# Rounding constant of a weight quantizer from a two-byte ScalarE magnitude, and nearly every second unit's second-half product in three passes

## Time and profile before

| | |
|---|---|
| time before, median of 3 runs | 833.17 us (832.89 to 833.23) |
| the profiled execution's own time | 833.1 us |
| its span, first to last instruction | 831.3 us |
| stage 1, up to the last hidden and project products | about 381 us |
| stage 2 | the rest |
| granted TensorE clock | 1.00 throughout |
| busy: PE, DVE, ACT, POOL | 825.8, 479.5, 345.9, 511.8 us |

### The profile page before, as it was taken

The page is one execution under the profiler, slowest core; times in us unless marked ns, Lnnn a source line. Parts: engine busy times, 40 slices in busy tenths (PEclk is TensorE's granted clock), DMA queues, the critical chain, the costliest instruction groups (busy, mean ns, idle before and its releaser), DMA issues.

```text
span 831.3 us, 10181 instructions
## 1 busy us (share of the span) xinstructions
PE 825.8 (99%) x3568; PEld 479.9 (58%) x3568; DVE 479.5 (58%) x499; ACT 345.9 (42%) x372; POOL 511.8 (62%) x238
## 2 busy tenths in 40 slices
PE   9999999999999999999999999999999999999998
PEld 5777777776767676765444444444444444444444
DVE  6989889788888888888553232323232323232322
ACT  7999999988888888973100000000000000000000
POOL 2899999899999999995983242424242423232322
PEclk9999999999999999999999999999999999999999
DMA  7988999877777877657974868686868686868682
GB/s 258 322 321 321 367 339 353 301 285 296 284 289 303 305 267 301 253 187 246 298 295 119 282 214 282 210 285 212 280 213 280 214 283 214 279 213 282 215 248 107
DMA packets 75008, 220.77 MB, mean 266 GB/s; under 512 B 37594, under 2 KB 40930, under 8 KB 55778
## 3 DMA queue, kind: packets, MB, share of 16 engines
q1 hardware_dynamic: 74080, 219.30, 74.5%
q10 hardware_dynamic: 898, 1.09, 0.4%
HBM read 143.04 MB, written 69.21 MB: 255 GB/s over the span
## 4 chain that ended last, share of the span: by engine, by line
PE 99%; issue 0%; POOL 0%; DVE 0%; ACT 0%; POOLq 0%
PE ps_h L1071 53%; PE ps_h L980 22%; PE ps_o L995 11%; PE ps_o L1011 8%; PE ps_o L1007 4%; PE ps_o L934 1%; PE ps_h L1047 0%; PE ps_o L1071 0%; PE ps_o L980 0%; PE ps_o L1065 0%; POOL time L518 0%; PE ps_o L940 0%; PE ps_h L1052 0%; DVE o_and_max L881 0%; ACT x_sb L702 0%
## 5 line engine op out<-in xcount | busy, mean ns | idle before, releaser
L1071 PE MATMUL ps_h<-wqT,x_sb 128*128 128x512 bf16 x1920 | 413.7, 378 | 0.2 <-ACT x_sb L702 0.2
L1071 PEld LDWEIGHTS ps_h<-wqT,x_sb 128*128 128x128 fp8e5 x1920 | 187.7, 98 | 224.4 <-ACT x_sb L702 0.3
L528 POOL TENSOR_TENSOR xl<-x_sb,xh 128x1024 fp32r<-128x1024 f32 x62 | 149.5, 2411 | 16.3 <-ACT xh L607 16.3
L980 PE MATMUL ps_h<-xh,whl 128*128 128x512 f32 x508 | 150.3, 417 | 0.4
L569 POOL TENSOR_TENSOR x_sb<-x_sb,bias_sb 128x2048 f32<-128x2048 f32 (+1 forms) x15 | 66.7, 4447 | 131.7 <-DMA x_sb<-in_x 131.7
L569 POOL TENSOR_TENSOR h<-h,bias_sb 128x2048 f32<-128x2048 f32 (+1 forms) x15 | 66.7, 4443 | 122.7 <-DMA h<-in_x 122.7
L881 DVE SCALAR_TENSOR_TENSOR o_and_max<-ps_h,scales,h 128x512 f32<-128x512 f32 (+1 forms) x59 | 44.0, 746 | 136.2 <-PE ps_h L1071 136.2
L881 DVE SCALAR_TENSOR_TENSOR o_and_max<-ps_h,scales,x_sb 128x512 f32<-128x512 f32 x59 | 44.2, 750 | 133.4 <-PE ps_h L1071 133.4
L980 PEld LDWEIGHTS ps_h<-xh,whl 128*128 128x128 f32 x508 | 94.2, 188 | 42.0 <-issue 21.7
L765 DVE SCALAR_TENSOR_TENSOR o_and_max<-ps_o,b_sb,steps 128x1024 f32<-128x1024 f32 (+1 forms) x65 | 82.2, 1264 | 29.0 <-PE ps_o L1011 27.1
L755 DVE TENSOR_TENSOR hl<-ps_h,hh 128x1024 fp32r<-128x1024 f32 x63 | 76.8, 1219 | 13.4 <-ACT ps_h L614 13.3
(11 more groups left out here) (101 smaller groups left out, 657.2 us busy)
## 6 DMA issues: line engine op xcount, KB each, us to landing
x_sb<-in_x SPq DMA_DIRECT2D x44, 1024.0 KB, 5.7
masked_out<-o_and_max SPq DMA_DIRECT2D x32, 1024.0 KB, 6.8
o_in<-masked_out SPq DMA_DIRECT2D x32, 1024.0 KB, 8.9
out<-o_and_max SPq DMA_DIRECT2D x27, 1024.0 KB, 5.1
wqT<-in_L_ffn_weight SPq DMA_DIRECT2D x23, 684.0 KB, 8.3
wt<-in_L_ffn_weight SPq DMA_DIRECT2D x40, 384.0 KB, 5.5
h<-in_x SPq DMA_DIRECT2D x14, 1024.0 KB, 7.2
whl<-split_w SPq DMA_DIRECT2D x18, 256.0 KB, 6.0
```

The source lines that it names most:

```text
L528: pool.tensor_tensor(xl[:, u % 2, :], x_cols(u), xh[:, u % 2, :].bitcast(fp32), ALU.subtract)\
L980: mm = nc.tensor.matmul(to[:, cols], whl[:, b % SLOTS_W, rows], xs[:, u % 2, cols], start=(k == 0), stop=(k == 2))
L1071: mm = nc.tensor.matmul(bank, q[:, k // 2, :, k % 2], wq[:, n, k, cols], start=(k == 0), stop=(k == KT - 1))
```

## The change

- The rounding constant comes another way. ACT's `scale_chunk` writes `wc = |wt * w_up|` in bf16, with `w_up` = `w_scale` * 2^20 (one small DVE operation more). DVE's `add_round_at` floors `wc` in place, as one contiguous run of 768 bf16 elements, and then makes `ws = wt * w_scale + wc` with one `scalar_tensor_tensor`, which reads `wt` and `wc` in SBUF. `exponents`, `round_at`, `wE` and POOL's addition (L535) go; POOL keeps the subtraction.
- `SPLIT_H1` has one unit more (27), and `QUANT` is one larger (27), so 34 chunks are early and nine late.
- `SPLIT_BEHIND`: the odd units from 29 to 61, 17 of them, run project1 in three passes too. ACT runs two Gelus for them (one to `hh1_behind`, one in place in PSUM); DVE, not POOL, makes the low half `hl1_behind` from PSUM right behind the mask, and scans `o` at the end of its iteration instead of ahead of the chunk. hidden(u+1, 1) waits for the low half.
- SP loads a chunk's buffer again after the DVE addition (`w_added`) instead of after ACT's scaling. ACT scales chunk 36 ahead of its copies at the beginning of stage 2. The late chunks are spread anew on DVE and POOL.

```diff
-    ROUND_AT = 1.5 * 2.0 ** 20
+    ROUND_AT = 2.0 ** 20
-    SPLIT_H1 = [u for u in range(2, 27)]
+    SPLIT_H1 = [u for u in range(2, 28)]
+    SPLIT_BEHIND = [u for u in range(29, UNITS - 2, 2)]
-    QUANT = SCANS + 2
+    QUANT = SCANS + 3
-    CHUNK_BEHIND = range(4, 12)
+    CHUNK_BEHIND = (2, 4, 5, 6, 7)
+        hh1_behind = sb_at("hh1_behind", [P, 2, UNIT], fp32r, h1_at)
+        hl1_behind = sb_at("hl1_behind", [P, UNIT], fp32r, raw_at)
...
@@ SyncE
                     if i >= 3:
-                        sp.wait_ge(w_scaled, i - 2)
+                        sp.wait_ge(w_added, i - 2)
                     load_chunk(i)
@@ GpSimd
             def round_chunk(i):
                 v, c = ws[:, i % 2, 0:chunk_cols(i)], wc[:, i % 2, 0:chunk_cols(i)]
-                pool.wait_ge(w_round_ready, i + 1)
-                pool.tensor_tensor(v, v, c, ALU.add).then_inc(w_added, 1)
                 pool.wait_ge(w_added, i + 1)
                 pool.tensor_tensor(wqT[:, CHUNK_AT[i]], v, c, ALU.subtract).then_inc(w_rounded, 1)
...
@@ ScalarE
                 act.wait_ge(h1_psum, u + k + 1)
+                if u in SPLIT_BEHIND:
+                    act.activation(hh1_behind[:, u % 2, :], ps_h[:, 1, :], ACT.Gelu, bias=hbias[:, 1, b:b + 1])
+                    act.activation(ps_h[:, 1, :], ps_h[:, 1, :], ACT.Gelu, bias=hbias[:, 1, b:b + 1])\
+                       .then_inc(h1_gelu, 1)
+                    return
...
-                act.activation(ws[:, i % 2, 0:chunk_cols(i)], wt[:, at:at + chunk_cols(i)], ACT.Copy, scale=w_scale)\
-                   .then_inc(w_scaled, 1)
+                act.activation(wc[:, i % 2, 0:chunk_cols(i)], wt[:, at:at + chunk_cols(i)], ACT.Abs, scale=w_up)\
+                   .then_inc(w_raised, 1)
...
+            scale_chunk(EARLY_CHUNKS + 2)
@@ VectorE
+            def split_h1_behind(u):
+                dve.wait_ge(h1_gelu, u + 1)
+                if u == SPLIT_BEHIND[0]:
+                    dve.wait_ge(wl_later, DIRECT - UPB)
+                dve.tensor_tensor(hl1_behind[:, :], ps_h[:, 1, :], hh1_behind[:, u % 2, :].bitcast(fp32), ALU.subtract)\
+                   .then_inc(hl1_behind_ready, 1)
...
+            def add_round_at(i):
+                c, at = wc[:, i % 2, 0:chunk_cols(i)], i % 3 * CHUNK
+                dve.wait_ge(w_raised, i + 1)
+                dve.tensor_scalar(c, c, 1.5 * E4M3_MIN_NORMAL * ROUND_AT, None, ALU.max).then_inc(w_floored, 1)
+                dve.wait_ge(w_floored, i + 1)
+                dve.scalar_tensor_tensor(ws[:, i % 2, 0:chunk_cols(i)], wt[:, at:at + chunk_cols(i)], w_scale, c,
+                                         ALU.mult, ALU.add).then_inc(w_added, 1)
...
                     mask_o(u - 1, start, 0, slice(0, UNIT))
+                    if u in SPLIT_BEHIND:
+                        split_h1_behind(u)
...
-                    scan_o(u - 1, 0, slice(0, UNIT))
+                    if u not in SPLIT_BEHIND:
+                        scan_o(u - 1, 0, slice(0, UNIT))
                 if 0 <= u - QUANT - 1 < EARLY_CHUNKS + 1:
-                    exponents(u - QUANT - 1)
-                if 0 <= u - QUANT - 1 < EARLY_CHUNKS:
-                    round_at(u - QUANT - 1)
+                    add_round_at(u - QUANT - 1)
                 if u + 1 < UNITS:
                     split_h_rest(u + 1)
+                if u in SPLIT_BEHIND:
+                    scan_o(u - 1, 0, slice(0, UNIT))
@@ TensorE
                     pe.wait_ge(h1_gelu, u)
+                    if u - 1 in SPLIT_BEHIND:
+                        pe.wait_ge(hl1_behind_ready, SPLIT_BEHIND.index(u - 1) + 1)
...
+                elif u in SPLIT_BEHIND:
+                    for j, (w, hs) in enumerate(((w2l1, hh1_behind[:, u % 2, :]), (w2h1, hh1_behind[:, u % 2, :]),
+                                                 (w2h1, hl1_behind))):
+                        for cols in halves:
+                            mm = nc.tensor.matmul(ps_o[:, u % 2, cols], w[:, :], hs[:, cols],
+                                                  start=False, stop=(j == 2))
```

More of the change, by code:

```diff
@@ L11, in adaln_ffn @@
     fp32r = mybir.dt.float32r
-    u16 = mybir.dt.uint16
     ALU, ACT, AX = mybir.AluOpType, mybir.ActivationFunctionType, mybir.AxisListType
@@ L30, in adaln_ffn @@
     E4M3_MAX, E5M2_MAX, EPS = 448.0, 57344.0, 1e-12
-    EXPONENT = 0x7F80
     E4M3_MIN_NORMAL = 2.0 ** -6
-    ROUND_AT = 1.5 * 2.0 ** 20
+    ROUND_AT = 2.0 ** 20
     assert C == P and UPB == 2 and HT == 2 and weight.shape == (P, WCOLS)
@@ L47, in adaln_ffn @@
     SLOTS = 5
-    CHUNK, CROWS = 768, 3
+    CHUNK = 768
     CHUNKS = -(-WCOLS // CHUNK)
-    QUANT = SCANS + 2
+    QUANT = SCANS + 3
     EARLY_CHUNKS = UNITS - 3 - QUANT
@@ L120, in adaln_ffn @@
         o_max = sb("o_max", [P, UNITS + 1], fp32)
-        scales = sb("scales", [P, 10], fp32)
+        scales = sb("scales", [P, 11], fp32)
         w_pmax, w_rec, w_scale, w_inv = (scales[:, k:k + 1] for k in range(4))
-        o_pmax, o_amax, o_rec, o_scale, o_inv, y_scale = (scales[:, k:k + 1] for k in range(4, 10))
+        o_pmax, o_amax, o_rec, o_scale, o_inv, y_scale, w_up = (scales[:, k:k + 1] for k in range(4, 11))
         wqT = sb("wqT", [P, WCOLS], bf16)
         x_sb = sb("x_sb", [P, 2, T], fp32)
+        raw_at = -(-nc.sbuf_base // 32) * 32
         raw = sb("raw", [P, SLOTS_W, HID], fp32)
+        assert SLOTS_W * HID == UNIT
         whl = sb("whl", [P, SLOTS_W, 2 * HID], fp32r)
@@ L137, in adaln_ffn @@
         hl = sb("hl", [P, 2, UNIT], fp32r)
+        h1_at = -(-nc.sbuf_base // 32) * 32
         h1 = sb("h1", [P, 2, UNIT], fp32)
@@ L146, in adaln_ffn @@
         ws = sb("ws", [P, 2, CHUNK], fp32)
-        wE = sb("wE", [P, CROWS * (CHUNK // CROWS + 2)], u16)
         wc = sb("wc", [P, 2, CHUNK], bf16)
@@ L236, in adaln_ffn @@
         hl1_ready = sem("hl1_ready")
+        hl1_behind_ready = sem("hl1_behind_ready")
         hl_ready = sem("hl_ready")
@@ L250, in adaln_ffn @@
         wt_loaded = [sem(f"wt_loaded{r}") for r in range(3)]
-        w_scaled = sem("w_scaled")
-        w_exponent = sem("w_exponent")
-        w_round_ready = sem("w_round_ready")
+        w_raised = sem("w_raised")
+        w_floored = sem("w_floored")
         w_added = sem("w_added")
@@ L299, in adaln_ffn @@
         o_row = ps_h[:, 1, 0:P]
[L301 to L307, removed]
         @block.sync
@@ L574, in _ @@
             add_bias(x2[0], FRONT)
-            for i in late[0:2]:
+            for i in late[0:3]:
                 round_chunk(i)
@@ L578, in _ @@
             add_bias(x2[1], FRONT)
-            for i in late[2:6]:
+            for i in late[3:7]:
                 round_chunk(i)
@@ L582, in _ @@
             add_bias(x2_more[0], FRONT)
-            for i in late[6:]:
+            for i in late[7:]:
                 round_chunk(i)
@@ L627, in scale_chunk @@
                 if i == 0:
-                    act.wait_ge(w_scale_ready, 1)
+                    act.wait_ge(w_scale_ready, 2)
                 if i >= 2:
@@ L705, in _ @@
             for i in range(EARLY_CHUNKS + 2, CHUNKS):
-                scale_chunk(i)
+                if i > EARLY_CHUNKS + 2:
+                    scale_chunk(i)
                 if UNITS - QUANT + 2 <= i + 3 < CHUNKS:
-                    act.wait_ge(w_scaled, i + 1)
+                    act.wait_ge(w_added, i + 1)
                     at = i % 3 * CHUNK
@@ L796, in weight_scale @@
                 dve.wait_ge(scale_step, 1)
+                dve.tensor_scalar(w_up, w_rec, E4M3_MAX * ROUND_AT, None, ALU.mult).then_inc(w_scale_ready, 1)
                 dve.tensor_scalar(w_scale, w_rec, E4M3_MAX, None, ALU.mult).then_inc(w_scale_ready, 1)
-                dve.wait_ge(w_scale_ready, 1)
+                dve.wait_ge(w_scale_ready, 2)
                 dve.reciprocal(w_inv, w_scale).then_inc(scale_step, 1)
@@ L867, in _ @@
             late = range(EARLY_CHUNKS, CHUNKS)
-            round_at(late[0])
             quantize(1, 1, True, slice(0, T))
@@ L873, in _ @@
             for i in late[1:4]:
-                exponents(i)
-                round_at(i)
+                add_round_at(i)
             dve.wait_ge(scale_step, 7)
@@ L902, in _ @@
                        .then_inc(y_ready, 1)
-                if y in CHUNK_BEHIND and 4 + CHUNK_BEHIND.index(y) < len(late):
+                if y in CHUNK_BEHIND:
                     i = late[4 + CHUNK_BEHIND.index(y)]
-                    exponents(i)
-                    round_at(i)
+                    add_round_at(i)
             def step2(i, last):
```

## The result

The changed kernel takes 857.17 us (median of 4 runs) against 833.03 of the kernel before in the same session: a ratio of 1.029, 95% interval 1.027 to 1.031, or 24.1 us more. The forecast was 846.5 us, with a range of 836 to 855. The sign was right and the size was not. The profiled execution has a span of 856.2 us, 24.9 more than before. Of all the executions in this document one stands apart: one of the last experiment's eleven took 1717 us, and the ratios leave it out.

A forecast was written before the change was run, and what follows sets the result against it. TensorE was taken to bound both stages; 17 pairs at +0.8 us (+13.6), unit 27 at -0.3 and the rest at nothing gave +13.3 on 833.1, so 846.5 us, with a range of 836 to 855.

The forecast's parts named there:

- PE's side: Stage 1, project1 on PE: three passes save 0.33 us a unit, at most 6.0 us over 18 units.
- rival A: Stage 1: the shared port doesn't matter, floor and addition aren't held; -3 to -6 us, 827 to 830; chance 0.16.
- The hold: Behind units, DVE: POOL's xl holds the floor 1.3 us; it ends 0.22 us after xl; 0.35 us when free.
- The pair: Stage 1, two units from 28 to 62: 12.6 us instead of 11.78, +0.8 each, 17 pairs.
- The rest at nothing: SP's chunk loads and queue: SP waits for the addition, about a unit later, with 11 us of cover; priced at 0.
- Stage 2 loses nothing else: it is PE's: Stage 2: beyond the late chunks no loss, since PE bounds it; priced at 0.
- Stage 2's late chunks: Stage 2, nine late chunks for eight on DVE: 0, at most +2 us; sign: idle PE after 390 us.
- B: Stage 1: only the addition is held, the floor is not; +0.4 us a pair, about +7, 840 us; chance 0.08.
- C: ACT, or SP's later chunk loads, becomes the bound: +8 us more, 855 us; chance 0.03.
- D: Stage 1: floor half held, gains pay for it; 833 us within 0.2%; chance 0.03.

The follow-up runs named there:

- the last experiment: The second experiment's kernel, but GpSimd rounds chunk 34 ahead of its first bias addition instead of behind it; 831.78 us, 0.9987 of the kernel before.
- the fourth experiment: The kernel before with only the 17 odd units 29 to 61 in three passes and the scan behind, old rounding kept; 831.00 us, 0.9976 of before.
- the sixth experiment: The first experiment's kernel, but ScalarE writes the magnitude in padded rows into ws, and VectorE's floor reads them and writes contiguous wc; 842.23 us, 1.012 of before.
- the first experiment: The changed kernel, but SyncE's last chunk load (chunk 38) is issued behind the first transpose; 848.88 us, 1.019 of the kernel before.
- second experiment: The first experiment's kernel, but VectorE's chunk floor and addition stand behind the scan and the low half hl in all units; 834.49 us, 1.0017 of before.

## Why the prediction was right and where it was wrong

- **PE's side, right in kind.** Three passes save 0.33 us a unit, and the other engines, not PE, set what comes of it. With nothing held, stage 1 gained 2.1 to 2.7 of the 6.0 us, a little less than rival A's 3 to 6.
- **The hold, right, and shown.** The floor was predicted at 0.35 free and 1.5 held (4.6 to 6.1), ending 0.22 us after xl. Measured: 0.35, 1.69, and 0.22. That it decides is shown by VectorE's order alone (848.9 to 834.5) and by the fourth experiment, where longer passes at the same place aren't held and cost nothing. That each of the two instructions is held by itself is shown for the floor by its own 1.69 us and for the addition by the sixth experiment, that GpSimd holds the floor by the last. One reading of the earlier trace rows was off: of mask, scan and low half only the scan lies inside xl there. The changed kernel shows the other two: most of `hl_behind` (292.70) and all of a mask (298.75) run beside an xl, and take their usual 1.21 and 1.28 us.
- **The pair, right, a term small.** 12.6 predicted, 12.68 measured. The chain held at each step: the floor ends at 6.10 us of the pair (6.1 predicted), `hl` at 8.28 (8.35), PE starts at 8.43 (8.4). What PE does from there took 4.25 us, not 4.18. With that and the rounding +0.8 a pair was taken and +0.90 measured; over 17 pairs this is the difference in stage 1, +13.3 predicted and +14.9 measured.
- **The failed step: "The rest at nothing: SP waits for the addition instead of the scaling, about a unit later".** I checked the steady state, where the buffer has 11 us of cover, and the buffer's reader, and not the last turn of the loop. There the awaited addition isn't a unit later but on the other side of the stage's end, and what pays isn't the chunk's reader but the store and the transpose queued behind on SP. Measured by the first experiment: 8.3 us. With it the sum would have been 833.1 + 13.3 + 8.3 = 854.7; with stage 1's measured 14.9, 856.3; with the next term, 857.1.
- **A second term at nothing: the maximum.** "Stage 2 loses nothing else: it is PE's" left out that VectorE, behind PE at the end of stage 1, brings the maximum later. PE waited 0.82 us for it, 0.8 us of the time.
- **Stage 2's late chunks, right.** 0, at most 2, was predicted; at most 0.3 remains in the first experiment. But the sign given for them, idle PE after 390 us, came from SyncE's queue.
- **Rivals.** A fell: the floor begins at 4.4 us of the pair, inside xl (3.5 to 5.9), and A's point was 3.45. B, the addition alone held, was priced at 840 as a whole; built as such it gave 842.2. C's bounds didn't appear, but its "SP's later chunk loads" named the right queue for the wrong reason, a late buffer. D fell.

## What to carry to other kernels

Before an instruction is moved to VectorE, or given a denser form, look at which of its forms GpSimd's running instruction holds up: the price is set by where the two meet, not by the instruction's own time, and putting it behind what others wait for can win all of it back. When a wait is moved to another semaphore, follow it through the last turn of the loop: who raises that count there, and what else stands in the same in-order queue.

## What the runs showed that I had not expected

- Padding in place doesn't keep the floor from being held (0.41 free, 1.77 held); only a source and a destination of different shape did (0.54, also inside xl). That form costs about 0.2 us against the contiguous 0.35. That source and destination are different tensors isn't enough: L784 went from `wE` to `wc` at 421.34 too, with 512 columns in one row on both sides, and took 1.61 us.
- A wait of TensorE of 6.4 us (changed kernel), and one of 2.2 us among other gaps (second experiment), were followed by a granted clock of 0.86 over the stretch of 24 to 25 us around them; with a wait of 0.9 us at that place (last experiment) the mean stayed 1.00.
